# Full attention in a two-layer kernel: causal mask by a matrix product, and another order of blocks and output tiles

## What is computed

```python
A_hidden = A.transpose(0, 2, 1, 3).reshape(b, s, H)      # A: result of the window attention
qa = (A_hidden @ Wqa.T + bqa).reshape(b, s, NH, HD).transpose(0, 2, 1, 3)
ka = (A_hidden @ Wka.T + bka).reshape(b, s, NH, HD).transpose(0, 2, 1, 3)
g = jnp.einsum('bhqd,bhkd->bhqk', qa, ka) * SCALE
causal = pos[:, None] >= pos[None, :]
g = jnp.where(causal[None, None], g, -jnp.inf)
pg = jax.nn.softmax(g, axis=-1)
out = jnp.einsum('bhqk,bhkd->bhqd', pg, A)
out = out.transpose(0, 2, 1, 3).reshape(b, s, H)
return out @ Wd.T + bd                                    # then x + s * gate
```

## Time and profile before

| | us |
|---|---|
| time, median of three runs (lowest to highest) | 2464.86 (2462.44 to 2468.89) |
| the profiled execution's own time | 2463.58 |
| its span on the slowest core (core 6 of 8) | 2462.0 |
| spans of the eight cores | 2452.4 to 2462.0 |
| TensorE matmuls busy, whole span | 1654.6 (67%) |
| VectorE busy | 1458.7 (59%) |
| ScalarE busy | 1174.5 (48%) |
| GpSimd busy | 285.3 (12%) |

### The profile page before, as it was taken

How to read it: one execution, slowest core, us unless ns; L and a number is a source line. 1 busy time by engine, 2 the same in 40 slices (tenths; PEclk the granted TensorE clock), 3 DMA queues, 4 the chain that set the end, 5 groups by cost and what they waited for, 6 DMA issues and landing times.

```text
span 2462.0 us, 22992 instructions; the slowest of 8 cores (2452.4 to 2462.0 us)
## 1 busy us (share of the span) xinstructions
PE 1654.6 (67%) x7301; PEld 643.9 (26%) x7431; DVE 1458.7 (59%) x1752; ACT 1174.5 (48%) x1289; POOL 285.3 (12%) x276
## 2 busy tenths in 40 slices
PE   0167357675655655608999997897479946777774
PEld 0022122222212221203444442232353311222221
DVE  8788699999659999313333016236652277755442
ACT  1582377776666767321111123123345534668771
POOL 1000144334120000110000000000020000010001
PEclk9978776677867866759999999899559957899997
DMA  7452310111241100264231021001121120110011
GB/s 163 111 103 39 56 26 15 24 20 26 67 114 29 20 7 0 81 140 90 54 68 33 1 43 22 5 13 22 22 53 31 30 43 27 43 52 18 35 35 60
DMA packets 103694, 113.23 MB, mean 46 GB/s; under 512 B 80148, under 2 KB 80564, under 8 KB 101496
## 3 DMA queue, kind: packets, MB, share of 16 engines
q1 hardware_dynamic: 91192, 71.05, 11.2%
q0 software_dynamic: 12384, 40.69, 10.1%
HBM read 115.96 MB, written 16.81 MB: 54 GB/s over the span
## 4 chain that ended last, share of the span: by engine, by line
PE 36%; DVE 26%; issue 17%; ACT 12%; DMA 4%; POOL 1%; SPq 1%; DVEq 0%; ACTq 0%; POOLq 0%
PE PS L1333 8%; DVE cs L923 5%; PE PS L1441 5%; PE PS L1374 5%; ACT pt L1745 4%; PE PS L1771 3%; PE PS L1547 2%; PE PS L1806 2%; DVE rf L1781 2%; DMA xres<-x 2%; PE PS L1730 2%; DVE rt L1463 2%; PE PS L1480 2%; ACT sqr L1474 1%; DVE nf L1779 1%
## 5 line engine op out<-in xcount | busy, mean ns | idle before, releaser
L1745 ACT ACTIVATE pt<-PS,negb 128x1024 bf16<-128x1024 f32 (+2 forms) x240 | 228.0, 1023 | 144.9 <-PE PS L1730 144.8
L953 PE MATMUL PS<-sq,bones 128*128 128x512 bf16 x252 | 97.6, 528 | 207.5 <-ACT sq L936 171.9
L1333 PE MATMUL PS<-xn_fm,wgu 128*128 128x512 bf16 x1003 | 221.6, 381 | 2.0 <-DVE um L1346 0.7
L1486 DVE TENSOR_REDUCE mx<-PS 16x1 f32<-16x1024 f32 x64 | 77.5, 1212 | 174.8 <-PE PS L1480 174.8
L788 PE MATMUL PS<-xn_fm,wz 128*128 128x512 bf16 x501 | 133.0, 421 | 31.9 <-SPq L111 26.6
L923 DVE TENSOR_TENSOR_SCAN cs<-vr,carr 128x1024 bf16<-128x1024 bf16 x64 | 148.9, 2369 | 0.0
L936 ACT ACTIVATE sq<-cs 128x1024 bf16<-128x1024 bf16 x128 | 127.8, 1047 | 40.7 <-DVE cs L923 40.7
L923 DVE TENSOR_TENSOR_SCAN cs<-vr 128x1024 bf16<-128x1024 bf16 x64 | 142.9, 2275 | 0.0
L1343 ACT ACTIVATE rl<-PS 128x1024 bf16<-128x1024 f32 x32 | 32.8, 1024 | 223.9 <-PE PS L1333 217.1
L1333 PEld LDWEIGHTS PS<-xn_fm,wgu 128*128 128x128 bf16 x1024 | 100.4, 98 | 122.9 <-issue 3.4
L1730 PE MATMUL PS<-RK,RV 64*128 64x512 bf16 (+3 forms) x640 | 96.2, 380 | 47.9 <-ACT pt L1745 46.5
(11 more groups left out here) (260 smaller groups left out, 3225.6 us busy)
## 6 DMA issues: line engine op xcount, KB each, us to landing
wz<-l_wz POOLq DMA_DIRECT2D x32, 384.0 KB, 4.7
xt<-x SPq DMA_DIRECT2D x8, 1024.0 KB, 6.7
xres<-x SPq DMA_DIRECT2D x16, 512.0 KB, 4.6
x<-sgt SPq DMA_DIRECT2D x16, 512.0 KB, 2.9
wgu<-l_wgu POOLq DMA_DIRECT2D x8, 1024.0 KB, 11.0
wp<-l_wproj POOLq DMA_DIRECT2D x32, 256.0 KB, 3.6
xo<-x SPq DMA_DIRECT2D x16, 512.0 KB, 4.2
out<-yo SPq DMA_DIRECT2D x16, 512.0 KB, 2.9
```

Of the source, the lines that this page charges most:

```text
L953: t = do("tensor", lambda e, _s=s2, _r=r: e.matmul(PM[:, _s * 512:(_s + 1) * 512], bones[:], sq[_r][k][:, _s * 512:(_s + 1) * 512], start= ...
L1333: g = (lambda e, _w=w, _f=f, _d=dc, _b=bb, _t=tt: e.matmul(PS[:, _b + _f * 512:_b + (_f + 1) * 512], _w[:, _d * 512 + _f * 128:_d * 512 + ...
L1745: e.activation(pt[_g][:, 0:_o], PS[:, _b:_b + _o], AF.Exp, bias=sb["negb2"][:, _h:_h + 1], scale=0.125))
```

## The change

Three things are changed, all in the full attention.

1. The causal mask. The constant `cmask` is now 0 where a key may be seen and -1e30 where not. For the key tiles on the diagonal the score matmul is split into the first 128 columns and the rest, and behind the first 128 of each head a matmul of the identity with `cmask` is summed onto them in PSUM. The VectorE products on the exponentials are gone. The exponential of a head waits for that head's last matmul.
2. The order of the blocks. First comes pair 0 of block 3, then pair 0 of block 0, pair 1 of block 3, pair 1 of block 0, and so on; then all pairs of block 2, then those of block 1. A table `SLOT` says which slot of `ofm` a block uses, and `nf`/`rf` take turns by finish.
3. The output tiles. Those of block 0 (0 to 3) stand behind the steps 1 to 4 of pair 0 of block 2, those of block 3 (12 to 15) behind step 1 of pairs 2 to 5 of block 2, those of block 2 (8 to 11) behind step 1 of pairs 1 to 4 of block 1, and those of block 1 (4 to 7) at the end.

```diff
-    c["c_cmask"] = np.triu(np.ones((128, 128), np.float32)).astype(BF16NP)
+    c["c_cmask"] = np.where(np.triu(np.ones((128, 128), np.float32)) > 0, 0.0,
+                            -1e30).astype(BF16NP)
...
+            diag = kt >= 4 * b
+            for lo, hi in ((0, 128), (128, w)) if diag else ((0, w),):
+                for r, (k, base) in enumerate(slots):
+                    if lo == hi:
+                        continue
+                    t = do("tensor", lambda e, _k=kt, _o=base + o, _q=b * 512 + off,
+                           _l=lo, _h=hi, _r=64 * r, _d=diag: e.matmul(
+                               PS[:, _o + _l:_o + _h],
+                               KA[_r:_r + 64, p * T + _k * 128:p * T + (_k + 1) * 128],
+                               QA[_r:_r + 64, p * T + _q + _l:p * T + _q + _h],
+                               start=True, stop=not _d or _l > 0,
+                               tile_position=(_r, 0)))
+                    if diag and lo == 0:
+                        t = do("tensor", lambda e, _o=base + o: e.matmul(
+                            PS[:, _o:_o + 128], sb["ident"][:], sb["cmask"][:],
+                            start=False, stop=True))
+                    t_sc[r] = t
...
-            need("scalar", t if r else t_even, t_pt[g])
+            need("scalar", t_sc[r], t_pt[g])
...
-            if 2 * k2 >= 4 * b:
-                need("vector", tok)
-                for _, _, _, o1 in blocks:
-                    tok = do("vector", lambda e, _g=g, _o=o1: e.tensor_tensor(
-                        pt[_g][:, _o:_o + 128], pt[_g][:, _o:_o + 128],
-                        sb["cmask"][:], ALU.mult))
...
-            q = p % 2
+            q = nfin[0] // 2 % 2
+            nfin[0] += 1
...
-                need("vector", v, t_wdm.get(b - 2))
-                t_fin[(b, p)] = do("vector", lambda e: e.tensor_tensor(
-                    ofm[b % 2][:, p * 512:(p + 1) * 512], nf[q][:], rf[q][:],
+                need("vector", v, t_wdm[SLOT[b]])
+                t_fin[(b, p)] = t_nf[q] = do("vector", lambda e: e.tensor_tensor(
+                    ofm[SLOT[b]][:, p * 512:(p + 1) * 512], nf[q][:], rf[q][:],
...
-    for b in range(4):
-        for p in range(8):
-            for k2 in range(2 * b + 2):
-                fresh = scores(p, b, k2)
-                for args in held:
-                    weigh(*args)
-                held = fresh
-            if b > 0 and p in (1, 2, 3, 4):
-                dense(4 * (b - 1) + p - 1)
+    blocks_of = [(b, p) for p in range(8) for b in (3, 0)]
+    blocks_of += [(b, p) for b in (2, 1) for p in range(8)]
+    dense_at = {(2, 0, 1): 0, (2, 0, 2): 1, (2, 0, 3): 2, (2, 0, 4): 3,
+                (2, 2, 1): 12, (2, 3, 1): 13, (2, 4, 1): 14, (2, 5, 1): 15,
+                (1, 1, 1): 8, (1, 2, 1): 9, (1, 3, 1): 10, (1, 4, 1): 11}
+    for b, p in blocks_of:
+        for k2 in range(2 * b + 2):
+            fresh = scores(p, b, k2)
+            for args in held:
+                weigh(*args)
+            held = fresh
+            if (b, p, k2) in dense_at:
+                dense(dense_at[(b, p, k2)])
     for args in held:
         weigh(*args)
-    for i in range(12, 16):
+    for i in range(4, 8):
         dense(i)
```

More of the change, by code:

```diff
@@ L1758, in emit_attn @@
     t_pt = [None] * NP
+    t_sc = [None, None]
+    SLOT = {0: 0, 3: 1, 2: 0, 1: 1}
+    nfin = [0]
     def weigh(h, b, g, blocks, tok):
@@ L1794, in dense @@
         b, c = i // 4, i % 4
-        need("sync", t_y.get(i - 1))
+        need("sync", t_y.get('last'))
         t_x1 = dma("sync", "s_xo", lambda e: e.dma_start(out=xo[:],
```

28 lines of the change are left out of this document (9 added, 19 removed).

## The result

The changed kernel is slower: its profiled execution took 2499.22 us, another undisturbed one 2503.4 us, against 2464.86 us before; the ratio to before is 1.0147 (95% interval 1.0119 to 1.0174), so 36 us. The median of the two is 2501.3 us. The forecast was 2487 us with a range of 2459 to 2505 us.

What follows compares the result with a forecast made beforehand. ScalarE was taken to bound blocks 3, 2 and 1, VectorE block 0. Couples end at 2187.8 us, first four tiles 2225.9, block 2 2335.8, block 1 2430.6, span 2485.4; plus 1.6 gives 2487 us, range 2459 to 2505.

Steps and rivals of the forecast that it cites:

- case (a): Rival on TensorE's diagonal steps: switching between 64-row and 128-row matmuls is hidden, 42 us less, 2445 us; chance 0.11.
- case (c): Rival in pairs of blocks 3 and 0: finishes do not queue, 5 us less eight times, 2447 us; chance 0.05.
- The switch: TensorE's diagonal steps: each change between 64-row score and 128-row mask matmuls costs 0.10 us, bounds 0 and 0.15.
- diagonal scores: Score and mask matmuls of a pair's two diagonal steps: 1.69 us until the value matmuls in the first, 1.26 in the second.
- The finishes: VectorE's copies, reciprocal and product per head pair: in blocks 3 and 0 they queue, the second starting copies 7.02 us later.
- The couple: One block-3 pair plus one block-0 pair: 26.3 us against 24.3 before, bounds 23.4 and 27.5.
- case (d): Clock stays low two steps after each bank wait: 1.2 us for eight pairs, 2497 us; chance 0.73 together with the forecast.
- central sum: The whole kernel's forecast, added up stage by stage: span 2485.4 us, profiled execution 2487 us.
- The output tiles: 4.3 us of TensorE each; the first four 6 to 7 us apart after some 4 us wait, fourth ending at 2225.9.
- Blocks 2 and 1: Ordinary pairs after the couples: 13.7 us in block 2, 9.7 in block 1, plus 4.3 us per output tile.
- The tail behind the last finish: From the start of the last finish to the end of the span: unchanged from before at 48.4 us.
- the chain followed through: Step-by-step timing of a pair's scores, exponentials and value matmuls with switches: block 2 needs 13.7 us, not 12.84.

Runs made afterwards that it cites:

- grouped masks: Mask matmuls of a step together behind unsplit scores: 2458.82 us, ratio 0.9977, with the change's order and tiles; 2442.61 us, ratio 0.9918, with the old ones.
- short reciprocal: The changed kernel with VectorE's reciprocal on only the first 128 of 512 columns: 2473.64 us, ratio 1.0033.
- the deferred one: New order with mask matmuls together behind unsplit scores; block-3 reciprocal and product moved behind the following block-0 pair's copies: 2437.40 us, ratio 0.9897.
- the filler matmuls: The changed kernel plus six unread 512-column matmuls behind step 1's scores of each block-3 pair but the first: 2488.73 us, ratio 1.0092.

## Why the prediction was right, and where it was off

**Direction and mechanism** were right: slower, by the switches and by finishes that queue. The case (a), switch hidden, would have shown masks 0.06 us from their neighbours; they stand 0.16 us apart. The case (c), no queue, would have shown less than 3 us of dry ScalarE a couple, and the start of the block-3 pair alone has 2.99.

**The switch** was taken as 0.10 us from the earlier trace rows and measured as 0.11. The diagonal scores came to 1.65 and 1.23 us for 1.69 and 1.26 predicted, ScalarE's dry time to 0.95 and 0.42 us for 1.1 and 0.6. The prediction put the switches at 42 us in all; the kernel with grouped masks and everything else of the change is 42 us faster. By parts it is 2.6 us for a couple (2.4 predicted), 1.4 us for a pair of block 2 (1.5) and 1.4 us for one of block 1 (1.4).

**The finishes** queued as predicted, 7.02 us apart. The short reciprocal took 28 us off and the deferred one 20, with different edits at the same place. Both numbers include clock that comes back with the shorter wait (0.89 for 0.81, and 0.92 for 0.82), so the queue and the low clock are not added up here.

**The couple** was 27.29 us and not 26.3. The term that was too small is the low clock: I had added 0.5 us, and the filler matmuls show 1.6 us. Seven times 1.0 is 7 us of the 12 us by which the sum of the profiled execution fell short (copies of the last block-3 finish start at 2194.35 for 2187.8, where those of the first started at 2003.3 for 2003.7). This is case (d), which the forecast held apart: 1.2 us on top of the 0.5, and 2497 us. The central sum was low because of the choice of the row. The earlier trace rows has a clock of 0.83, and I read from it a cost per pair of block 1. But its window lies over two pairs: taken apart, the one of 10.33 us has 0.74 and the 12.84 us one of block 2 has 0.94, and the second lost time as well (below). After the wait of each couple TensorE has whole steps of block 3, in which S and W together last 1.6 us of ScalarE's 2.0 at full clock; at half clock they take 2.8 us and outlast it, until the clock is back.

**The output tiles** were placed right: first one after a wait of 3.35 us (predicted some 4), the next 6.9 us apart (6 to 7), and 19.7 us from the end of the first tile to the end of the fourth (19.6). But the first was costed at 4.3 us, the price at full clock, and ran mostly at 1.2 GHz for 6.5 us behind its own wait. That is 2.2 us, and with 0.2 us of a later start it puts the fourth tile's end at 2234.9 for 2225.9.

**Blocks 2 and 1.** The ordinary pairs were a little shorter than predicted (13.51 for 13.7, 9.55 for 9.7), but four were not ordinary: 14.55 us for the last of block 2 and 11.70 us where the block changes, 15.45 us for a pair of block 1 with a tile and 12.02 us for the last. Together they are 6.6 us over the predicted 13.7, 9.7, 14.0 and 9.7, and the others give some 1.3 us back: from the fourth tile's end to the first copy of the last finish, at 2451.28, the sum was 5.3 us short. The windows over the intervals show what the four have in common (columns as in the earlier trace rows; the pair where the block changes and the last one):

```profile
2354.37:2366.07 11.70, 10.12 (x46) 3.43 (x46) 6.80 (x7) 7.25 (x9) 0.00 (x0) 0.71 0.01 2
2442.21:2454.23 12.02, 9.24 (x36) 3.38 (x36) 6.80 (x6) 3.85 (x5) 0.00 (x0) 0.50 0.00 0
```

The granted clock is 0.71 and 0.50 here, 0.88 and 0.89 in the other two, and 1.00 in all eleven others behind the first pair of block 2. The sum had every pair of blocks 2 and 1 at full clock; why just these four fall is open. The tail behind the last finish was 46.4 us and not 48.4, which happened to hide 2 us of the shortfall.

**The base of block 2** hid a second error. I compared with the 12.84 us of the earlier trace rows and so read 0.7 to 0.9 us as the price of the mask. The kernel with VectorE's mask in the new order has 12.20 at a granted clock of 1.00, and the one with grouped masks 12.15; the 12.84 ran at 0.94. So it held 0.6 us of low clock, and the interleaved mask costs 1.3 us a pair there. The forecast of 13.7 did not rest on that base, since it came from the chain followed through.

**What I had not thought of** is that the two halves don't add: 28 and 37 us alone, 36 together. The prediction followed the change through as a whole; a forecast as the sum of the halves, each costed against before, would have given 65 us.

## What to carry to other kernels

Matmuls of different tiling belong in groups: price one switch from a place where the two shapes already meet, and count switches, not columns. Before two kinds of work are interleaved "to hide" one under the other, write down when the shared in-order engine comes free for the second of them, and let it first do what others wait for (here: empty the bank), then its long operation. And where TensorE waits long enough for the granted clock to fall, price the steps behind the wait from rows that run at the low clock, each row over one pair and not over two.

## What the runs showed of the hardware

- A switch between 64-row and 128-row matmuls costs 0.11 us at 2.4 GHz (0.16 us between neighbours whose columns take 0.053) and the same 0.11 us at 1.2 GHz (0.22 us, columns 0.107): here it does not scale with the granted clock.
- Six matmuls whose result is thrown away, 0.2 us each at full clock, put into TensorE's waits lifted the granted clock from 0.81 to 0.98 over the stretch and made the kernel 13 us faster.
- VectorE's reciprocal takes 3.35 us for 128 x 512 and 0.95 us for 128 x 128. A copy of 128 x 512 from PSUM takes 0.68 us, a fifth of the reciprocal, and a copy of 64 x 512 takes 0.69 us, as long as that of 128 partitions: this is why the whole bank comes out in half the time.
- The granted clock and the length of a pair go together in blocks 2 and 1 of the changed kernel: an ordinary pair of block 2 takes 13.51 us at 1.00 and 14.55 us at 0.88, and one of block 1 with an output tile 13.86 us at 1.00 and 15.45 us at 0.89.
